# A fused RWKV attention and feed-forward block: the first tile's products with the state moved behind the second scores

## The chip, the cores and the metric

One core of a Trainium2 chip. The metric is device microseconds of one execution, median of three runs.

## The reference

Input x is 4 sequences of 2048 tokens with 512 channels. Two residual blocks follow each other, each on a layer norm of its input:

- Attention with a decaying state, 32 heads of 16 channels. r, k, v and a gate g are projections (512 x 512) of the normalized tokens mixed with the token before. A sequence is cut into chunks of 64 tokens. Per chunk and head: `att = (r k) * w_mat; y = att v + (r state) * wb; state = ws * state + (k * wk) v`. Then y is normalized per head, multiplied by silu(g) and projected by Wo.
- Feed-forward: `gelu(x W0' + b0) W1' + b1`, 512 to 2048 to 512, with half-precision roundings.

## The kernel before, in words

The 8192 tokens go through in 32 steps (n = 0 to 31) of 256 tokens, a step being two tiles (t) of 128 tokens, or four chunks (c) of 64. Three more steps drain the pipeline. Step n does the attention of block n, the tail (gate, Wo) of block n-1 and the feed-forward of block n-2; the down projection of block n-3 ends in it as well. Float32 operands are split into two halves of 16 bits (hi and lo), and a product is three matmuls (`PASSES`).

Each engine has one instruction stream, written out by hand, and works it off in order; semaphores order the engines among each other (`eng.wait_ge(s, count)`). From step 3 on the streams of VectorE and ScalarE are `dve_steady` (L1447) and `act_steady` (L1788); steps 0 to 2 use `dve_step` (L1534) and `act_step` (L1849). TensorE's is `pe_step` (L1174) for all of them. In steps 0 and 1 TensorE also prepares the feed-forward weights in 16 pieces (`pe_prepare`, L830).

What the change and the prediction speak of:

- The feed-forward pieces: `pe_up` (L1061), 16 matmuls each, counted 0 to 7 in the code ("up 4" to "up 7" here; the sixth piece is up 5). Pieces alternate between two banks of `F`, and from up 2 on each waits for the gelu of the piece two before it: `eng.wait_ge(s_h, NH * f + 2 * (j - 2) + 2)` (L1072). The gelus are ScalarE's `act_gelu` (L1773, L1785).
- The scores of a chunk: `pe_scores` (L940, L954), 32 small matmuls into `sc`; "second scores" are those of chunk 1. VectorE weighs them (`dve_weigh`, L1345, L1350), ScalarE makes the high half (`act_weights_hi`, L1736), VectorE the low half (`dve_weights_lo`, L1356), and TensorE multiplies weights with values (`pe_att_v`, L960, L976 and L979) per tile.
- The state: `pe_kv` (L1005) makes both chunks' products k v of a tile. VectorE masks each (`dve_state`, L1359, L1367) into `kv` and adds it to the faded state S (L1382). ScalarE makes the high half of S (`act_state_hi`, L1738), GpSimd the low half (`pool_state_lo`, L1985, L1988; semaphore `s_Sl`).
- "Products with the state": `pe_from_state` (L984, L995), 48 small matmuls per tile into `FROM_STATE`, the columns 0 to 255 and 768 to 1023 of the three banks of `YT`. `dve_take_y` (L1393) adds them to what `pe_att_v` left in `FROM_CHUNK`, the other columns. Before the change chunk 1's product k v lies in columns 768 to 1023 (`kv_place`, L1001).
- The gate's projection, in two halves: `pe_G` (L1031). The tail of block n-1: VectorE multiplies with the gate (`dve_gated`, L1311), ScalarE makes the high halves (`act_gated_hi`, L1724, "gated high halves"), GpSimd the low ones (`pool_gated_lo`, L1979), TensorE projects (`pe_Wo`, L1041).
- The next block's mixes: `dve_mix` (L272) and their high halves, `act_mix_hi` (L329, L335).

Of the kernel before, what the change touches and what calls it, by code (L numbers as in the profile page):

```python
# [8 lines left out]
ALU = mybir.AluOpType  # L9
# [4 lines left out]
C = 512  # L14
H, N = 32, 16
G = C // P
HID = 2048
Q = 64
BT, NT = 256, 2
NCH = BT // Q  # L20
# [16 lines left out]
def due(count):  # L37

    return not isinstance(count, int) or count > 0
# [55 lines left out]
def program(nc, ctx, a, consts, x, out, wd, nb):  # L95
# [67 lines left out]
    Y = YT[:, 0:2, :]  # L163
    T32 = YT[:, 2, :]
# [566 lines left out]
    kv = sb("kv", [P, C // 2])  # L731
    S = sb("S", [P, C // 2])
    Shl = sb("Shl", [P, 2, 2, C // 2], F16)
    yi = sb("yi", [P, C])
# [249 lines left out]
    def pe_from_state(eng, n, t):  # L984

        if n == 0 and t == 0:
            eng.wait_ge(s_zero, 2)
        if due(NCH * n + 2 * t + 1):
            eng.wait_ge(s_Sl, NCH * n + 2 * t + 1)
        for g in range(G):  # L990
            for i, (a, b) in enumerate(PASSES):
                for p in range(2):
                    for cc in range(2):
                        at = P * t + Q * cc
                        mm = eng.matmul(FROM_STATE[Q * cc:Q * cc + Q, rows_of(g, p).start // Q, Q * g:Q * g + Q],  # L995
                                        rT[rows_of(g, p), a, g, at:at + Q], Shl[rows_of(g, p), cc, b, Q * g:Q * g + Q],
                                        start=(i == 0), stop=(i == 2))
                        if g == G - 1 and i == 2 and p == 1:
                            mm.then_inc(s_in, 1)

    def kv_place(c):  # L1001

        return Y[:, 1, C // 2:C] if c % 2 else T32[:, 0:C // 2]

    def pe_kv(eng, n, t, ahead):  # L1005

# [24 lines left out]
    def pe_G(eng, n, half, ahead):  # L1031
        if half == 0:
            pe_mixed(eng, n, 3)
            eng.wait_ge(s_rl, 2 * n + 1)
            if ahead:
                eng.wait_ge(s_xT, NT * (n + 1) + 1)
        else:
            eng.wait_ge(s_gT, 2 * n + 1)
        pe_project_T(eng, B, G_, n, 3, half).then_inc(s_pG, 1)
# [134 lines left out]
    def pe_step(eng, n):  # L1174
        att_n, tail, ff, ahead, late = in_step(n)
        if n == nb:
            pe_after_attention(eng, n)
            return
        if n == nb + 2:
            pe_last_down(eng)  # L1180
            return
        if att_n and n != 1:
            pe_mixed(eng, n, 0)
            pe_K(eng, n, 0)
        if late:
            pe_down(eng, n - 3, 4)
        if att_n:
            pe_K(eng, n, 1)
        if late:
            pe_down(eng, n - 3, 5)  # L1190
        if att_n:
            pe_mixed(eng, n, 1)
            pe_R(eng, n, 0)
        if late:
            pe_down(eng, n - 3, 6)
        if att_n:
            pe_R(eng, n, 1)
            if n == 0:
                pe_piece_mean(eng, 0)
        if late:  # L1200
            pe_down(eng, n - 3, 7)
        if att_n:
            pe_mixed(eng, n, 2)
            pe_V(eng, n, 0)
            if n == 2:
                pe_V(eng, n, 1)
                pe_yT(eng, n)
            if n < STEADY:
                pe_next_X(eng, n)
            if n == 1:  # L1210
                pe_piece_mean(eng, 1)
            pe_prepare(eng, n, "X")
        if ff:
            pe_up(eng, n, 0)
        if att_n and n != 2:
            pe_V(eng, n, 1)
        if n == 1:
            pe_yT(eng, n)
        if att_n:
            pe_prepare(eng, n, "V1")  # L1220
        if ff:
            pe_up(eng, n, 1)
        if n > 2 and tail and not y_by_dma(n - 1):
            pe_yT(eng, n)
        if ff:
            pe_up(eng, n, 2)
        if ff:
            pe_up(eng, n, 3)
        if att_n:
            pe_scores(eng, n, 0)  # L1230
            pe_prepare(eng, n, "sc0")
            pe_kv(eng, n, 0, n < STEADY)
            pe_G(eng, n, 0, n < STEADY)
            pe_prepare(eng, n, "G0")
        if ff:
            pe_up(eng, n, 4)
        if att_n:
            pe_scores(eng, n, 1)
            pe_prepare(eng, n, "sc1")
        if ff:  # L1240
            pe_up(eng, n, 5)
        if att_n:
            pe_G(eng, n, 1, n < STEADY)
            pe_prepare(eng, n, "G1")
        if ff:
            pe_up(eng, n, 6)
        if att_n:
            pe_att_v(eng, n, 0)
        if ff:
            pe_up(eng, n, 7)  # L1250
        if att_n:
            pe_from_state(eng, n, 0)
            pe_scores(eng, n, 2)
            pe_prepare(eng, n, "sc2")
        if tail:
            pe_Wo(eng, n, 0)
            pe_prepare(eng, n, "Wo0")
        if ff:
            pe_down(eng, n - 2, 0)
        if att_n:  # L1260
            pe_kv(eng, n, 1, n < STEADY)
            pe_scores(eng, n, 3)
            pe_prepare(eng, n, "sc3")
        if n == 0:
            pe_mixed(eng, 1, 0)
            pe_K(eng, 1, 0)
        if ff:
            pe_down(eng, n - 2, 1)
        if tail:
            pe_Wo(eng, n, 1)  # L1270
        if ff:
            pe_down(eng, n - 2, 2)
        if att_n:
            pe_att_v(eng, n, 1)
            pe_from_state(eng, n, 1)
        if ff:
            pe_down(eng, n - 2, 3)
# [75 lines left out]
    def dve_weights_lo(eng, n, c):  # L1353
        for x in range(2):
            eng.wait_ge(s_ah, 8 * n + 2 * c + x + 1)
            eng.tensor_tensor(att[:, c % 2, 1, C * x:C * x + C], att32[:, x, :], att[:, c % 2, 0, C * x:C * x + C],  # L1356
                              ALU.subtract).then_inc(s_al, 1)

    def dve_state(eng, n, c):  # L1359
        eng.wait_ge(s_kv, NCH * n + c + 1)  # L1360
        if due(NCH * n + c):
            eng.wait_ge(s_S, NCH * n + c)
        dst = kv[:, :].rearrange("p (g c) -> p g c", g=G)
        src = kv_place(c).rearrange("p (g c) -> p g c", g=G)
        mask = headmask[:, :].unsqueeze(1).to_broadcast([P, G, 4 * N])
        if c < NCH - 1:
            eng.tensor_tensor(dst, src, mask, ALU.mult).then_inc(s_km, 1)  # L1367
        else:
            eng.scalar_tensor_tensor(out=dst, in0=src, scalar=flag[:, n + 1:n + 2], in1=mask,
                                     op0=ALU.mult, op1=ALU.mult).then_inc(s_km, 1)  # L1370
        eng.wait_ge(s_km, NCH * n + c + 1)
        fading = ws
        if c == NCH - 1:
            eng.wait_ge(s_wsf, n + 1)
            fading = wsf
        if due(NCH * n + c):
            eng.wait_ge(s_Sl, NCH * n + c)
        else:
            eng.wait_ge(s_zero, 1)
        for g in range(G):  # L1380
            at = slice(Q * g, Q * g + Q)
            last = eng.scalar_tensor_tensor(out=S[:, at], in0=S[:, at], scalar=fading[:, g:g + 1],  # L1382
                                            in1=kv[:, at], op0=ALU.mult, op1=ALU.add)
        last.then_inc(s_S, 1)

    def dve_gate(eng, n, half):
# [6 lines left out]
    def dve_take_y(eng, n, t):  # L1393
        eng.wait_ge(s_in, NCH * n + 2 * t + 2)
        eng.wait_ge(s_av, NCH * n + 2 * t + 2)
        if due(NT * n + t):
            eng.wait_ge(s_gs, NT * n + t)
        for x in range(2):
            at = slice(C // 2 * x, C // 2 * x + C // 2)
            last = eng.tensor_tensor(yi[:, at].rearrange("p (k a d) -> p a k d", a=2, d=N),  # L1400
                                     FROM_STATE[:, :, P * x:P * x + P].rearrange("p a (k d) -> p a k d", d=N)[:, ::1 - 2 * x],
                                     wb[:, H // 2 * x:H // 2 * x + H // 2].rearrange("p (k a) -> p a k", a=2).unsqueeze(3).to_broadcast(
                                         [P, 2, H // 4, N]), ALU.mult)
        last.then_inc(s_yi, 1)
        eng.wait_ge(s_yi, NT * n + t + 1)
        if due(NT * n):
            eng.wait_ge(s_yT, NT * n)
        halves = FROM_CHUNK.rearrange("p k (q b d) -> p k q b d", q=8, b=2)
        dst = y[:, t, :].rearrange("p (k q d) -> p k q d", k=2, q=8)
        sums = yi[:, :].rearrange("p (k q d) -> p k q d", k=2, q=8)  # L1410
        eng.tensor_tensor(sums, halves[:, :, :, 1, :], sums, ALU.add).then_inc(s_ylo, 1)
        eng.wait_ge(s_ylo, NT * n + t + 1)
        eng.tensor_tensor(dst, halves[:, :, :, 0, :], sums, ALU.add).then_inc(s_y, 1)
# [374 lines left out]
    def act_steady(eng, n, ahead):  # L1788
# [24 lines left out]
        act_gate(eng, n, 0)  # L1813
        act_state_hi(eng, n, 0)
        act_gated(eng, n - 1)
        act_weights_hi(eng, n, 1)
        act_gelu(eng, n, 4)
        act_gated_hi(eng, n - 1)
        if ahead:
            act_mix_hi(eng, n + 1, 0)  # L1820
# [436 lines left out]
```

## Time and profile before

| | |
|---|---|
| median of 3 runs | 2046.94 us (2045.29 to 2048.67) |
| profiled execution, its own time | 2050.78 us |
| profiled execution, span | 2049.0 us, granted clock 0.993 |
| TensorE busy | 1999.8 us (98%), 27206 matmuls |
| TensorE weight loads busy | 1424.3 us (70%) |
| VectorE busy | 1738.7 us (85%) |
| ScalarE busy | 1293.0 us (63%) |
| GpSimd busy | 317.5 us (15%) |
| chain that ended last | TensorE 81%, SyncE's queue 4%, VectorE 4%, ScalarE 4%, DMA 3%, issue 2% |
| granted TensorE clock over 40 slices | 0.8 in the first, 0.9 or more in all others |

Busy time is the union of an engine's instructions. The chain is followed back from the last instruction, at each step to what released it. A matmul's end is modelled, so TensorE is timed here by the starts of its instructions.

### The profile page before, as it was taken

The page shows a single profiled execution, that of the slowest core. Times are in us where ns is not written, and L with a number is a line of the kernel's source. Part 1 is how long each engine was busy: PE and PEld are TensorE (multiplying, and loading weights), DVE is VectorE, ACT ScalarE, POOL GpSimd, SP SyncE. Part 2 cuts the span into 40 slices and gives each one's busy share as a digit, 9 for nine tenths or more (in the row PEclk, how much of TensorE's full clock was granted, in tenths as well). Part 3 has the DMA queues.
Part 4 walks back from the last instruction along what each step waited for, and adds up shares of the span by engine and source line. Part 5 has one row for each costly group of instructions (what it writes and reads, how often), then busy time and mean ns, then how long its engine had stood idle before and what let it go on. Part 6 is the DMA issues. An engine that isn't in the chain of part 4 may idle for free.

```text
span 2049.0 us, 64453 instructions
## 1 busy us (share of the span) xinstructions
PE 1999.8 (98%) x27206; PEld 1424.3 (70%) x27206; DVE 1738.7 (85%) x3687; ACT 1293.0 (63%) x2081; POOL 317.5 (15%) x329
## 2 busy tenths in 40 slices
PE   5889999999999999999999999999999999999999
PEld 4767667777666777766777766667776677777676
DVE  7778889888888888888988888888888898888771
ACT  7775566676555677656667656667765666766452
POOL 1011111111111111111111111111111111111110
PEclk8999999999999999999999999999999999999999
DMA  6776666777666677766667766667777666776656
GB/s 217 161 193 194 177 178 182 199 197 196 177 194 171 189 198 195 185 190 189 173 194 202 199 174 186 181 181 202 192 195 184 191 180 185 199 202 177 181 175 191
DMA packets 403216, 385.42 MB, mean 188 GB/s; under 512 B 256880, under 2 KB 304112, under 8 KB 402928
## 3 DMA queue, kind: packets, MB, share of 16 engines
q1 hardware_dynamic: 401296, 381.12, 68.1%
q8 instruction: 215, 3.52, 0.7%
q14 instruction: 73, 0.60, 0.1%
q10 hardware_dynamic: 1632, 0.18, 0.1%
HBM read 232.32 MB, written 22.54 MB: 124 GB/s over the span
## 4 chain that ended last, share of the span: by engine, by line
PE 81%; SPq 4%; DVE 4%; ACT 4%; DMA 3%; issue 2%; POOL 0%; ACTq 0%; DVEq 0%
PE F L1149 19%; PE F L1086 16%; PE B L892 9%; PE B L1053 8%; PE sc L892 7%; PE YT L924 6%; PE YT L892 3%; DMA y<-ygT 3%; PE YT L976 3%; SPq L2044 2%; PE sc L954 2%; PE YT L995 2%; PE YT L1086 1%; PE F L847 1%; PE YT L1025 1%
## 5 line engine op out<-in xcount | busy, mean ns | idle before, releaser
L1149 PE MATMUL F<-ring,hT 128*128 128x512 f16 x1984 | 467.7, 379 | 0.5 <-issue 0.5
L1149 PEld LDWEIGHTS F<-ring,hT 128*128 128x128 f16 x1984 | 189.1, 98 | 198.4 <-issue 0.8
L1086 PE MATMUL F<-xT,kept 128*128 128x256 f16 x2400 | 276.8, 273 | 2.0 <-issue 1.2
L892 PE MATMUL B<-mix,WT 128*128 128x256 f16 x2304 | 267.5, 273 | 0.0
L1785 ACT ACTIVATE hT<-F,b,f_rho 128x256 f16<-128x256 f32 x480 | 243.4, 560 | 37.8 <-PE F L1086 37.7
L1086 PEld LDWEIGHTS F<-xT,kept 128*128 128x128 f16 x2400 | 234.6, 98 | 42.1 <-issue 2.6
L892 PEld LDWEIGHTS B<-mix,WT 128*128 128x128 f16 x2304 | 222.7, 98 | 33.3 <-DVE gT L1389 0.3
L279 DVE SCALAR_TENSOR_TENSOR mixf<-dx,maa,xnT 128x256 f32<-128x256 f32 x512 | 238.7, 527 | 0.1
L1742 ACT ACTIVATE Shl<-S 128x256 f16<-128x256 f32 x128 | 53.1, 415 | 236.2 <-PE YT L995 125.8
L1988 POOL TENSOR_TENSOR Shl<-S,Shl 128x256 f16<-128x256 f32 x128 | 89.2, 697 | 708.5 <-ACT Shl L1742 702.1
L1736 ACT ACTIVATE att<-att 128x512 f16<-128x512 f32 x256 | 147.5, 624 | 67.7 <-DVE att L1350 67.7
L339 DVE TENSOR_TENSOR mix<-mixf,mix 128x1024 f16<-128x1024 f32 x128 | 184.1, 1438 | 3.2 <-ACT mix L335 2.2
L892 PE MATMUL sc<-mix,WT 128*128 128x256 f16 x1536 | 180.4, 275 | 3.0 <-PEq L577 3.0
L1356 DVE TENSOR_TENSOR att<-att 128x512 f16<-128x512 f32 x256 | 166.8, 693 | 17.2 <-ACT att L1736 17.0
L924 PE MATMUL YT<-WT,mix 128*128 128x512 f16 x768 | 178.6, 383 | 1.3 <-DVE mix L339 0.9
L1086 PE MATMUL F<-xT,ring 128*128 128x256 f16 x1440 | 172.5, 273 | 4.1 <-ACT hT L1785 4.1
L1053 PE MATMUL B<-WT,yg 128*128 128x512 f16 x768 | 176.5, 379 | 0.0
L1350 DVE TENSOR_TENSOR att<-sc,wmask 128x512 f32<-128x512 f32 x256 | 164.3, 684 | 13.3 <-PE sc L954 13.1
L892 PEld LDWEIGHTS sc<-mix,WT 128*128 128x128 f16 x1536 | 151.0, 99 | 34.6 <-issue 3.6
L1993 POOL TENSOR_TENSOR x<-e,x 128x512 f32<-128x512 f16 x62 | 70.7, 1161 | 578.0 <-DVE e L1429 578.0
L1086 PEld LDWEIGHTS F<-xT,ring 128*128 128x128 f16 x1440 | 135.3, 98 | 23.3 <-issue 6.4
L335 ACT ACTIVATE mix<-mixf 128x1024 f16<-128x1024 f32 x128 | 134.6, 1051 | 5.1 <-DVE mixf L279 4.2
(208 smaller groups left out, 3108.6 us busy)
## 6 DMA issues: line engine op xcount, KB each, us to landing
ring<-w_dram SPq DMA_DIRECT2D x352, 512.0 KB, 3.7
kx<-kT SPq DMA_DIRECT2D x96, 256.0 KB, 3.8
rx<-rT SPq DMA_DIRECT2D x96, 256.0 KB, 4.5
xa<-in_L_attn_x SPq DMA_DIRECT2D x32, 512.0 KB, 5.0
vbd<-vN SPq DMA_DIRECT2D x256, 64.0 KB, 2.1
x<-in_L_attn_x SPq DMA_DIRECT2D x32, 512.0 KB, 5.0
out<-x SPq DMA_DIRECT2D x31, 512.0 KB, 3.5
kept<-in_L_ffn_W SPq DMA_DIRECT2D x5, 512.0 KB, 12.0
```

What stands on the lines that cost most here:

```text
L279: last = eng.scalar_tensor_tensor(out=mixf[:, m % 2, g, :], in0=dx[:, g, :], scalar=maa[:, m, g:g + 1], in1=xnT[:, g, 1:BT + 1], op0=ALU.m ...
L335: eng.activation(mix[:, m % 2, 0, :, :], mixf[:, m % 2, :, :], ACT.Copy).then_inc(s_mh, 1)
L339: eng.tensor_tensor(mix[:, m % 2, 1, :, :], mixf[:, m % 2, :, :], mix[:, m % 2, 0, :, :], ALU.subtract).then_inc(s_ml, 1)
L892: mm = eng.matmul(out[:, gg * BT:(gg + 1) * BT], WT[:, w, a, kk, rows(g)], mix[:, m % 2, b, kk, :], start=(i == 0 and kk == 0), stop=(i == ...
L924: mm = eng.matmul(Y[:, t, :], mix[:, 0, a, kk, rows(t)], WT[:, V_, b, kk, :], start=(i == 0 and kk == 0), stop=(i == 2 and kk == G - 1))
L1053: mm = eng.matmul(B[:, :], yg[:, a, kk, rows(t)], WT[:, O_, b, kk, :], start=(i == 0 and kk == 0), stop=(i == 2 and kk == G - 1))
L1086: mm = eng.matmul(up_place(f, j)[:, i * BT:(i + 1) * BT], w, xT[:, :, kk, :], start=(kk == 0 and a == 0), stop=(kk == G - 1 and a == 1))
L1149: mm = eng.matmul(F[:, t, :], hT[:, k, rows(t)], ring[:, use % RING, i, a * C:(a + 1) * C], start=(k == 0 and a == 0), stop=(k == NH - 1 a ...
L1350: eng.tensor_tensor(att32[:, x, :], sc[:, x, :], wmask[:, 8 * x:8 * x + 8, :].rearrange("p q i -> p (q i)"), ALU.mult).then_inc(s_am, 1)
L1356: eng.tensor_tensor(att[:, c % 2, 1, C * x:C * x + C], att32[:, x, :], att[:, c % 2, 0, C * x:C * x + C], ALU.subtract).then_inc(s_al, 1)
L1736: eng.activation(att[:, c % 2, 0, C * x:C * x + C], att32[:, x, :], ACT.Copy).then_inc(s_ah, 1)
L1785: eng.activation(hT[:, k, :], up_place(f, j)[:, i * BT:(i + 1) * BT], ACT.Gelu, bias=b0[:, k:k + 1], scale=f_rho[:, j:j + 1]).then_inc(s_h, 1)
```

## The change

- `pe_step`: the second scores go from behind up 4 to behind up 5, and the first tile's products with the state from behind up 7 to right behind the second scores. Up 6 and up 7 follow each other, and weights times values of the first tile comes behind up 7.
- `kv_place`: chunk 1's product k v goes to columns 256 to 511, out of `FROM_STATE`.
- `dve_state`: chunk 1's product is masked right behind chunk 0's fade, into the first half of `yi`; its fade stays where it was (`dve_fade`). `dve_take_y` of the first tile waits for that fade.
- `pe_from_state`: the first tile's also waits for chunk 1's mask.
- `act_steady`: gelu 4 goes ahead of the second scores' weights.

```diff
 def pe_from_state(eng, n, t):
-        if due(NCH * n + 2 * t + 1):
-            eng.wait_ge(s_Sl, NCH * n + 2 * t + 1)
+        if t == 0:
+            eng.wait_ge(s_km, NCH * n + 2)
+        eng.wait_ge(s_Sl, NCH * n + 2 * t + 1)
 def kv_place(c):
-        return Y[:, 1, C // 2:C] if c % 2 else T32[:, 0:C // 2]
+        return Y[:, 0, C // 2:C] if c % 2 else T32[:, 0:C // 2]
 def pe_step(eng, n):
             pe_up(eng, n, 4)
-        if att_n:
-            pe_scores(eng, n, 1)
-            pe_prepare(eng, n, "sc1")
         if ff:
             pe_up(eng, n, 5)
         if att_n:
+            pe_scores(eng, n, 1)
+            pe_from_state(eng, n, 0)
+            pe_prepare(eng, n, "sc1")
             pe_G(eng, n, 1, n < STEADY)
             pe_prepare(eng, n, "G1")
         if ff:
             pe_up(eng, n, 6)
+            pe_up(eng, n, 7)
         if att_n:
             pe_att_v(eng, n, 0)
-        if ff:
-            pe_up(eng, n, 7)
-        if att_n:
-            pe_from_state(eng, n, 0)
             pe_scores(eng, n, 2)
+    def masked(c):
+        return yi[:, 0:C // 2] if c == 1 else kv[:, :]
 def dve_state(eng, n, c):
+        if c == 1:
+            dve_fade(eng, n, c)
+            return
...
+        dve_fade(eng, n, c)
+        if c == 0:
+            eng.wait_ge(s_kv, NCH * n + 2)
+            if due(n):
+                eng.wait_ge(s_gs, NT * n)
+            eng.tensor_tensor(masked(1).rearrange("p (g c) -> p g c", g=G),
+                              kv_place(1).rearrange("p (g c) -> p g c", g=G), mask, ALU.mult).then_inc(s_km, 1)
+    def dve_fade(eng, n, c):
...
-                                            in1=kv[:, at], op0=ALU.mult, op1=ALU.add)
+                                            in1=masked(c)[:, at], op0=ALU.mult, op1=ALU.add)
 def dve_take_y(eng, n, t):
+        if t == 0:
+            eng.wait_ge(s_S, NCH * n + 2)
 def act_steady(eng, n, ahead):
         act_gated(eng, n - 1)
+        act_gelu(eng, n, 4)
         act_weights_hi(eng, n, 1)
-        act_gelu(eng, n, 4)
         act_gated_hi(eng, n - 1)
```

## Rows read from the trace of the kernel before

**Rows 1.** Waits of TensorE, 255 to 1960 us: total, times, longest.
```profile
PE F L1086 <- ACT hT L1785: 4.1, 8, 0.7
```
**Rows 2.** Timeline of TensorE, step 22: start, length, engine, line, form, count.
```profile
1403.96 0.45 PE L954 MATMUL sc<-rx,kx 64*64 64x64 f16 x32
...
1409.26 0.45 PE L954 MATMUL sc<-rx,kx 64*64 64x64 f16 x32
1409.64 1.92 PE L1086 MATMUL F<-xT,ring 128*128 128x256 f16 x16
1411.40 2.78 PE L892 MATMUL B<-mix,WT 128*128 128x256 f16 x24
1414.02 1.91 PE L1086 MATMUL F<-xT,ring 128*128 128x256 f16 x16
1415.86 0.22 PE L976 MATMUL YT<-vbd,att 128*64 128x64 f16 x2
...
1416.98 1.92 PE L1086 MATMUL F<-xT,ring 128*128 128x256 f16 x16
1418.83 0.58 PE L995 MATMUL YT<-Shl,rT 64*64 64x64 f16 x48
1419.23 0.46 PE L954 MATMUL sc<-rx,kx 64*64 64x64 f16 x32
1419.63 2.76 PE L1053 MATMUL B<-WT,yg 128*128 128x512 f16 x12
...
1464.01 0.45 PE L954 MATMUL sc<-rx,kx 64*64 64x64 f16 x32
```
**Rows 3.** Timeline of ScalarE, step 22, from the gated high halves to gelu 5.
```profile
1413.19 1.16 ACT L1729 ACTIVATE yg<-ygT 128x512 f16<-128x512 f32 x2
1414.23 1.06 ACT L335 ACTIVATE mix<-mixf 128x1024 f16<-128x1024 f32 x1
1415.18 1.02 ACT L1785 ACTIVATE hT<-F,b,f_rho 128x256 f16<-128x256 f32 x2
```
**Rows 4.** Timeline of VectorE, step 22.
```profile
1404.46 1.29 DVE L1350 TENSOR_TENSOR att<-sc,wmask 128x512 f32<-128x512 f32 x2 [0.28 <-PE sc L954]
...
1410.29 1.28 DVE L1350 TENSOR_TENSOR att<-sc,wmask 128x512 f32<-128x512 f32 x2
1411.49 1.29 DVE L1315 TENSOR_TENSOR ygT<-ygT,gT 128x512 f32<-128x512 f32 x2
```
**Rows 5.** Timeline of GpSimd, step 22.
```profile
1409.48 0.83 POOL L1988 TENSOR_TENSOR Shl<-S,Shl 128x256 f16<-128x256 f32 x1 [5.99 <-ACT Shl L1742]
```
**Rows 6.** Timeline of ScalarE, step 26: its gelu 5.
```profile
1656.79 1.00 ACT L1785 ACTIVATE hT<-F,b,f_rho 128x256 f16<-128x256 f32 x2
```
**Rows 7.** Timeline of TensorE, step 26: second scores and up 7.
```profile
1649.53 0.44 PE L954 MATMUL sc<-rx,kx 64*64 64x64 f16 x32
...
1658.00 1.92 PE L1086 MATMUL F<-xT,ring 128*128 128x256 f16 x16
```
**Rows 8.** Timeline of GpSimd, steps 0, 1 and 2: low half of the state.
```profile
84.90 0.67 POOL L1988 TENSOR_TENSOR Shl<-S,Shl 128x256 f16<-128x256 f32 x1 [14.30 <-ACT Shl L1742]
...
147.00 1.12 POOL L1988 TENSOR_TENSOR Shl<-S,Shl 128x256 f16<-128x256 f32 x1
...
204.64 1.12 POOL L1988 TENSOR_TENSOR Shl<-S,Shl 128x256 f16<-128x256 f32 x1
```
**Rows 9.** Timeline of TensorE, steps 0, 1 and 2.
```profile
72.42 2.04 PE L847 MATMUL F<-xT,kept 128*128 128x128 f32 x8 [2.27 <-ACT vw L828]
...
83.34 1.13 PE L847 MATMUL F<-xT,kept 128*128 128x128 f32 x8 [0.83 <-ACT kept L862]
...
142.53 1.13 PE L847 MATMUL F<-xT,ring 128*128 128x128 f32 x8 [0.83 <-ACT ring L862]
...
202.85 2.78 PE L892 MATMUL B<-mix,WT 128*128 128x256 f16 x24
```
**Rows 10.** Busy times in a window: length, engines with counts, PEclk, DMA share, GB/s.
```profile
72.40:75.80 3.40, 3.38 (x17) 3.34 (x18) 3.40 (x9) 1.29 (x3) 0.00 (x0) 0.50 0.98 108
```

More of the change, by code:

```diff
@@ L1362, in dve_state @@
             eng.wait_ge(s_S, NCH * n + c)
-        dst = kv[:, :].rearrange("p (g c) -> p g c", g=G)
+        if c == 1:
+            dve_fade(eng, n, c)
+            return
+        dst = masked(c).rearrange("p (g c) -> p g c", g=G)
         src = kv_place(c).rearrange("p (g c) -> p g c", g=G)
```

## The prediction

> **What bounds the kernel now.** I read the page's engine shares and its chain that ended last first: TensorE is busy 98% of the span and holds 81% of the chain, so the kernel is its in-order queue, and any wait put into that queue is added to the time. Next the waits of TensorE over the 28 steps n = 3 to 30, which are alike: 8 waits, 4.1 us in all, each of a feed-forward piece for a gelu that must empty the PSUM bank it will overwrite [rows 1]. So there is almost nothing to win by removing waits, and the change must be read as a new order in a full queue. For that I took one undisturbed step, n = 22, engine by engine: the reader is to see TensorE without a gap [rows 2], and beside it VectorE and ScalarE, whose order is fixed too and runs only a little ahead of it [rows 3, 4]. The step lasts 60.05 us (1403.96 to 1464.01).
>
> **The change part by part, in step 22.** Times count from the start of the second scores before the change (1409.26).
>
> *TensorE's order.* Before: second scores, up 5, gate half, up 6, weights times values, up 7, products with the state, third scores, Wo. After: up 5, second scores, products with the state, gate half, up 6, up 7, weights times values, third scores, Wo. No matmul is added or taken away. Up 5 takes 1.76 (1409.64 to 1411.40), the gate half 2.62, an up piece ahead of a large group 1.75 (its 1.76, rounded down), one ahead of a small group 1.85 (1416.98 to 1418.83), weights times values 1.12, the group of products and scores 0.40 + 0.40 [rows 2]. If nothing waits, the new order has the second scores at 1.76, the gate half at 2.56, up 6 at 5.18, up 7 at 6.93, weights times values at 8.78, third scores at 9.90 and Wo at 10.30. Before, Wo began at 10.37. So the regrouping alone gives 0.07 us a step: one group of small matmuls less has to be entered and left.
>
> The row for that: an up piece that is followed by a small group takes 0.09 longer than one that isn't [rows 2]. The Trainium skill, TensorEngine Tiling (Array Packing), section Key Properties, says that changing the tiling mode drains the engine. By that rule fewer changes of mode mean less time, and the change would be a gain; the trace agrees in sign.
>
> *The moved VectorE work.* The mask of chunk 1's product (0.42 us, same size) moves ahead of the mixes; it has its own destination, so nothing is computed twice. It makes VectorE reach the gate half 0.42 later, but it then still waits for the second scores: it would be ready at 1410.29 + 0.42, 1.45 after the mark, and the scores let it start at 2.26 (below). Cover 0.8 us, cost nothing.
>
> *The new waits of the products.* They need the low half of the state from GpSimd: ready at 1409.48 + 0.83, so at 1.05 after the mark, wanted at 2.16 [rows 5, 2]. Cost nothing in such a step; the mask they also wait for is earlier still.
>
> *What the second scores now hold up.* This is where it goes wrong. Up 7 writes the bank of up 5, so it waits for gelu 5. By `act_steady` after the change ScalarE runs gelu 4, the weights of the second scores, the gated high halves, the next block's mix, gelu 5 (the last three in [rows 3]); the edit swaps only the first two. The gated high halves wait for VectorE's gating, which stands in VectorE's queue behind the weighing of the second scores [rows 4]. So gelu 5 hangs on the second scores, which are now 1.76 later, though nothing in it needs them. Step by step: the weighing starts 0.50 after its scores start (1404.46 against 1403.96) [rows 2, 4], at 2.26. Gating starts 1.20 later (1410.29 to 1411.49), at 3.46, and takes 1.29, to 4.75. Take 0.05 for the signal, between no time and 0.1: high halves at 4.80. From there the spacings of the rows: 1.04 to the mix, 0.95 to gelu 5, 1.02 for gelu 5 itself, so it ends at 7.81, and up 7 starts at 7.85. It could have started at 6.93: TensorE waits 0.92. Before, gelu 5 ended at 1416.20 and up 7 started at 1416.98, so there were 0.78 to spare; both sides of the slack move against it. From up 7 on: 1.85 + 1.12 + 0.40 to Wo, at 11.22 against 10.37, **+0.85 us a step**. Later in the step nothing pays it back: Wo and the down pieces have no waits to shorten [rows 1].
>
> *Steps in which ScalarE is late.* In 8 of the 28 [rows 1] ScalarE got to its gated work late and up 6 waited for gelu 4, which is why gelu 4 is put ahead of the weights: that wait goes, 4.1 us. But what is ahead of gelu 5 is the same work in another order. In step 26 it ends at 1656.79 + 1.00 as before [rows 6], so up 7 starts at about 1657.84 instead of 1658.00 [rows 7], and from there to Wo it is 3.37 now and was 2.65 (1416.98 to 1419.63): +0.56.
>
> Sum of the steady steps: 20 x 0.85 + 8 x 0.56 = **21.5 us**.
>
> *Steps 0, 1 and 2.* There the products' wait is not covered. The low half of the state is ready at 85.57, 148.12 and 205.76 (start and duration of GpSimd's row; in steps 1 and 2 it also stands behind the gated low halves) [rows 8]. What TensorE now does after the second scores began at 83.34, 142.53 and 202.85 [rows 9]; with the products between (0.5) it begins at 86.1, 148.7 and 206.3, so 2.8, 6.1 and 3.4 later. Off go the products at their old place, 0.5 each as an estimate (0.40 and 0.09 of [rows 2]). That is 2.3 + 5.6 + 2.9 = **10.8 us**. The chain of waits runs through TensorE, ScalarE and VectorE there with little idle, so I take all of it; bounds 0 (all absorbed) and 14 (nothing taken off).
>
> *The clock.* After an idle time of 2.27 TensorE started at 72.42, and the stretch 72.4 to 75.8 had a granted clock of 0.50 [rows 9, 10]: 1.2 instead of 2.4 GHz, so about 1.7 us of 3.4 are lost. The new idle times are about 3.1, 6.5 and 2.9 us long. Bounds 0 and 3 x 1.7; I take two of the three, **3.4 us**. The 0.9 us of the steady steps should do nothing: the waits before were up to 0.7 [rows 1] and the page has full clock throughout.
>
> Sum: 21.5 + 10.8 + 3.4 = 35.7. The profiled execution (2050.78 by its own time) would become 2086.5. It lies 3.8 above the median of the runs, 2046.94, to which the sum is added for the forecast: **2082.6 us**.
>
> **The rivals.**
> 1. *Only the steady wait shows.* The early steps' idle is taken back by waits behind it, where ScalarE, VectorE and GpSimd catch up. For: the chain there changes engine every few microseconds. Against: TensorE's share of it is large, and its next steps start late. 21.5 alone: 2068.
> 2. *The wait feeds on itself.* ScalarE gets to its work late in every step, as in step 26, because transfers shift with the longer step. There gelu 5 ended 8.26 after the start of the second scores (1649.53) [rows 6, 7]; with 0.05 for the signal up 7 then starts at 8.31, not 7.85. 20 x 0.46 = 9.2 more, with the whole sum 44.9: 2092. Against: the late steps come from a DMA ahead of the moved work, and a longer step gives it more time.
> 3. *Faster: only the regrouping counts.* Mechanism: fewer groups of small matmuls, at 0.07 a step, and up 6 no longer waits. 28 x 0.07 + 4.1 = 6: 2041. It holds from the point at which gelu 5 ends by 6.9 after the mark, 0.9 earlier than worked out, and the early steps cost nothing. For it speaks 0.09 in the rows; against it the fixed order of ScalarE. This is the case that the skill's rule on modes leads to.
> 4. *A wash*: the steady steps gain 6 as in the third and the early steps pay 10.8: 2052 at most, about no change.
>
> **How the numbers follow.** Forecast 0.60, rival 1 0.18, rival 2 0.12, rival 3 0.05, rival 4 0.05. The forecast's own range is 2074 to 2089: steady 18 to 23, early 8 to 14, clock 0 to 5. The range of 8 in 10 takes in rivals 1 and 2, less about 0.08 at their far ends: 2062 to 2093. About 0.2% (4.1 us) can be told from no change. Faster 0.04, same 0.05, slower 0.91.
>
> **What would show it.** In the waits of TensorE after: up pieces waiting for gelu some 28 times, 0.7 to 0.95 each, 20 to 30 us in all, where 8 waits had 4.1. In a step: the wait stands ahead of up 7, none ahead of the products, and gelu 5 ends 0.05 before up 7 starts. ScalarE idle ahead of the gated high halves, with VectorE's gating as releaser. In steps 0 to 2: the products wait for GpSimd's low half. The period of an undisturbed step: 60.9. I am wrong if up 7 follows up 6 without a gap (then gelu 5 doesn't hang on the second scores), or if the products wait for the state in steady steps.

## The result

The changed kernel takes 2083.0 us (median of 6 runs, 2082.48 to 2085.58), the kernel before 2048.03 us (6 runs): ratio 1.0174, 95% interval 1.0163 to 1.0185. It is 35 us slower; 35.7 us were forecast. The profiled execution took 2082.48 us by its own time (span 2080.7 us, before 2049.0).

The page of the changed kernel, its engine shares: about as much TensorE work as before (1999.8 us, 98%) in a longer span.

```profile
PE 2001.7 (96%) x27206; PEld 1428.6 (69%) x27206; DVE 1746.3 (84%) x3687; ACT 1296.4 (62%) x2081; POOL 331.3 (16%) x329
```

The waits of TensorE from 250 to 2000 us, the steady steps. L1087 is the feed-forward piece, L1801 the gelu, L996 the products with the state, L2004 GpSimd's low half of the state. [rows 1] had 4.1 us in 8 waits:

```profile
PE F L1087 <- ACT hT L1801: 24.6, 28, 1.1
PE YT L996 <- POOL Shl L2004: 0.2, 1, 0.2
```

And from 60 to 260 us, steps 0 to 2, the first row of the answer:

```profile
PE YT L996 <- POOL Shl L2004: 11.9, 3, 6.6
```

So both waits are where the prediction put them. Step 22 after the change, TensorE, to be held against [rows 2]:

```profile
1427.71 0.44 PE L954 MATMUL sc<-rx,kx 64*64 64x64 f16 x32
...
1433.00 1.91 PE L1087 MATMUL F<-xT,ring 128*128 128x256 f16 x16
1434.84 0.44 PE L954 MATMUL sc<-rx,kx 64*64 64x64 f16 x32
1435.11 0.62 PE L996 MATMUL YT<-Shl,rT 64*64 64x64 f16 x48
1435.67 2.79 PE L892 MATMUL B<-mix,WT 128*128 128x256 f16 x24
1438.30 1.91 PE L1087 MATMUL F<-xT,ring 128*128 128x256 f16 x16
1441.06 1.91 PE L1087 MATMUL F<-xT,ring 128*128 128x256 f16 x16 [0.86 <-ACT hT L1801]
...
1488.77 0.45 PE L954 MATMUL sc<-rx,kx 64*64 64x64 f16 x32
```

VectorE in the same step, against [rows 4]: the weighing waits for the second scores, the gating follows.

```profile
1435.33 1.29 DVE L1348 TENSOR_TENSOR att<-sc,wmask 128x512 f32<-128x512 f32 x2 [0.89 <-PE sc L954]
1436.54 1.28 DVE L1313 TENSOR_TENSOR ygT<-ygT,gT 128x512 f32<-128x512 f32 x2
```

ScalarE, against [rows 3]: idle ahead of the gated high halves until VectorE's gating, then the mix and gelu 5.

```profile
1437.91 1.15 ACT L1745 ACTIVATE yg<-ygT 128x512 f16<-128x512 f32 x2 [0.63 <-DVE ygT L1313]
1438.97 1.04 ACT L335 ACTIVATE mix<-mixf 128x1024 f16<-128x1024 f32 x1
1439.92 1.00 ACT L1801 ACTIVATE hT<-F,b,f_rho 128x256 f16<-128x256 f32 x2
```

The reader is to see one chain: scores 1434.84, weighing 1435.33, gating 1436.54 to 1437.82, high halves 1437.91, mix, gelu 5 to 1440.92, up 7 at 1441.06. By the spacing of [rows 2] up 7 was wanted 1.75 after up 6, at 1440.05, so TensorE lost 1.01; the row's 0.86 counts from the modelled end of up 6.

Step 22 lasts 61.06 us here, 0.08 more than an undisturbed step of the changed kernel, and that 0.08 lies ahead of up 4 (which starts 3.54 after the first scores, 3.46 in step 22 before the change). Two first scores that are 60.98 apart, of steps 24 and 25:

```profile
1549.85 0.45 PE L954 MATMUL sc<-rx,kx 64*64 64x64 f16 x32
...
1610.83 0.45 PE L954 MATMUL sc<-rx,kx 64*64 64x64 f16 x32
```

Steps 0 to 2, TensorE, the products with the state:

```profile
83.38 0.57 PE L996 MATMUL YT<-Shl,rT 64*64 64x64 f16 x48 [3.21 <-POOL Shl L2004]
...
148.81 0.85 PE L996 MATMUL YT<-Shl,rT 64*64 64x64 f16 x48 [6.55 <-POOL Shl L2004]
...
213.61 0.57 PE L996 MATMUL YT<-Shl,rT 64*64 64x64 f16 x48 [2.11 <-POOL Shl L2004]
```

The granted clock behind these waits, by windows (length, then busy time of TensorE, its weight loads, VectorE, ScalarE and GpSimd, then PEclk):

```profile
84.90:88.30 3.40, 3.40 (x22) 3.15 (x20) 0.27 (x2) 0.49 (x1) 0.00 (x0) 0.50 0.09 27
146.30:153.20 6.90, 4.39 (x66) 4.29 (x67) 2.71 (x6) 0.06 (x1) 2.37 (x2) 0.51 0.02 6
214.60:218.00 3.40, 3.40 (x19) 2.42 (x17) 1.93 (x6) 0.76 (x2) 0.00 (x0) 0.50 0.02 5
```

The second of these stretches begins inside the wait, which ends at 148.81, so TensorE has only 4.39 us of work in it. The wait of 2.27 us in step 0, behind which the kernel before had half clock ([rows 9], [rows 10]), is there after the change too, but the clock behind it is 1.00 (71.7 to 76.0), and the same 8 matmuls take 1.13 us instead of 2.04:

```profile
71.72 1.13 PE L847 MATMUL F<-xT,kept 128*128 128x128 f32 x8 [2.27 <-ACT vw L828]
```

Counted by the starts of the first scores, steps 3 to 30 take 1709.2 us together, 1690.0 before: +19.2. Steps 0 to 2 take 61.83, 72.61 and 64.43, before 60.57, 65.02 and 60.41: +12.9. The start is 0.7 earlier and the end 0.3 longer: 31.7, the difference of the two spans. The medians differ by 3.3 more than these two executions. Step 0 of the kernel before can account for most of that: in the eight executions of this document that have TensorE's old order there, it takes 57.7 to 57.9 us in four, with full clock at 72 us, and 60.0 to 60.6 in four, with half clock there, and this execution is one of the latter.

### The profile page after: what moved, and what is told of

Read it like the earlier page. It is cut to its first block, busy times and chain, and to the rows that moved or that the text cites. A ratio compares the mean times of both kernels' runs of the same rounds, so it can differ in the third digit from the quotient of the medians.

```text
span 2080.7 us, 64546 instructions
## 1 busy us (share of the span) xinstructions
PE 2001.7 (96%) x27206; PEld 1428.6 (69%) x27206; DVE 1746.3 (84%) x3687; ACT 1296.4 (62%) x2081; POOL 331.3 (16%) x329
## 4 chain that ended last, share of the span: by engine, by line
PE 82%; DVE 5%; ACT 4%; issue 3%; DMA 1%; SPq 1%; POOL 0%; ACTq 0%; DVEq 0%
PE F L1150 20%; PE F L1087 17%; PE B L892 8%; PE B L1054 8%; PE sc L892 8%; PE YT L924 7%; PE YT L892 4%; PE YT L976 2%; PE sc L954 2%; DVE ygT L1313 1%; ACT mix L335 1%; PE F L847 1%; PE YT L1087 1%; PE YT L1026 1%; ACT hT L1801 1%
## 5 line engine op out<-in xcount | busy, mean ns | idle before, releaser
L1087 PE MATMUL F<-xT,kept 128*128 128x256 f16 x2400 | 276.8, 273 | 2.0 <-issue 1.2
L1801 ACT ACTIVATE hT<-F,b,f_rho 128x256 f16<-128x256 f32 x480 | 244.3, 563 | 38.1 <-PE F L1087 38.0
L1087 PEld LDWEIGHTS F<-xT,kept 128*128 128x128 f16 x2400 | 234.6, 98 | 42.1 <-issue 2.7
L2004 POOL TENSOR_TENSOR Shl<-S,Shl 128x256 f16<-128x256 f32 x128 | 96.0, 750 | 715.0 <-ACT Shl L1758 715.0
L1087 PE MATMUL F<-xT,ring 128*128 128x256 f16 x1440 | 171.6, 272 | 24.9 <-ACT hT L1801 24.9
L1054 PE MATMUL B<-WT,yg 128*128 128x512 f16 x768 | 176.5, 379 | 0.0
L1354 DVE TENSOR_TENSOR att<-att 128x512 f16<-128x512 f32 x256 | 166.4, 692 | 10.8 <-ACT att L1752 10.7
L1087 PEld LDWEIGHTS F<-xT,ring 128*128 128x128 f16 x1440 | 138.7, 98 | 48.1 <-issue 32.4
```

Source lines behind the costliest of these rows:

```text
L1054: mm = eng.matmul(B[:, :], yg[:, a, kk, rows(t)], WT[:, O_, b, kk, :], start=(i == 0 and kk == 0), stop=(i == 2 and kk == G - 1))
L1087: mm = eng.matmul(up_place(f, j)[:, i * BT:(i + 1) * BT], w, xT[:, :, kk, :], start=(kk == 0 and a == 0), stop=(kk == G - 1 and a == 1))
L1801: eng.activation(hT[:, k, :], up_place(f, j)[:, i * BT:(i + 1) * BT], ACT.Gelu, bias=b0[:, k:k + 1], scale=f_rho[:, j:j + 1]).then_inc(s_h, 1)
```

## The experiments

The theory: gelu 5 stands on ScalarE behind work that hangs on the second scores, and these now come one feed-forward piece later; in steps 0 to 2 the products with the state wait for GpSimd. The rivals: the new order costs something by itself (the products ahead of the gate half, or up 7 right behind up 6), or the idle time is there whatever the order. Line numbers shift by some lines with the edits; medians of the kernel before differ by up to 4.5 us between the groups of runs, so the ratios decide.

**Gelu 5 first.** The changed kernel with

```diff
         act_gelu(eng, n, 4)
+        act_gelu(eng, n, 5)
         act_weights_hi(eng, n, 1)
         act_gated_hi(eng, n - 1)
         if ahead:
             act_mix_hi(eng, n + 1, 0)
-        act_gelu(eng, n, 5)
```

> The changed kernel with one edit on ScalarE: gelu 5 directly behind gelu 4, ahead of the second scores' weights and the gated high halves. Theory (gelu 5 hangs on the second scores through the weighing, the gating and the gated high halves): TensorE's wait ahead of up 7 goes, an undisturbed step goes from 60.98 us to about 60.0, 28 steps give back 27 us, 2056 us; steps 0 to 2 stay as slow. Rival (the next wait stands right behind, since the gated high halves and the low halves for Wo now come after one gelu more): the wait moves ahead of Wo or of weights times values, over 2075 us.

2061.53 us, 1.0058 of before (1.0039 to 1.0078). Up 6 and up 7 now run as one piece of 32 matmuls. TensorE in a step of this run, 1425 to 1431 us:

```profile
1425.99 3.66 PE L1087 MATMUL F<-xT,ring 128*128 128x256 f16 x32
```

No up piece waits for a gelu any more; an undisturbed step takes 60.02. But the rival has a share. The waits of TensorE in the steady steps (L1054 is Wo, L1403 the gate half that VectorE reads out of the bank that Wo writes):

```profile
PE B L1054 <- DVE gT L1403: 6.8, 9, 0.8
PE YT L996 <- POOL Shl L2004: 1.4, 3, 0.5
```

The 9 steps are those in which ScalarE starts its gated work over 0.7 us late; their wait has moved on. The two rows come to 8.2 us, enough for the 5.5 us above the 2056 expected (4 by the ratio, since the kernel before was 1.5 slower in these runs).

**The old order in steps 0 to 2.** The changed kernel with the products and the second scores at their old places where `n < STEADY`:

```diff
+        old = n < STEADY
+        if att_n and old:
+            pe_scores(eng, n, 1)
+            pe_prepare(eng, n, "sc1")
         if ff:
             pe_up(eng, n, 5)
-        if att_n:
+        if att_n and not old:
             pe_scores(eng, n, 1)
             pe_from_state(eng, n, 0)
-            pe_prepare(eng, n, "sc1")
...
+            if old:
+                pe_from_state(eng, n, 0)
             pe_scores(eng, n, 2)
```

> The changed kernel with TensorE's old order in steps 0 to 2 alone (second scores behind up 4, products with the state behind up 7). Theory: the products no longer wait for GpSimd's low half of the state there; the three steps took 12.9 us longer in the trace, so 2070 us, and the steady steps stay at 60.98. Rival (that idle time is mostly taken back or is the clock's and comes anyway): 2078 us or more.

2070.22 us, 1.0096 (1.0080 to 1.0112), with 28 waits of 24.6 us in the steady steps as before the edit. The early cost is as large as the trace showed: 12.8 us by the medians, 16 by the ratios. Step 0 itself differs between executions (57.9 here, 60.6 in the kernel before), so a single pair of traces gives the cost to about 3 us: steps 0 to 2 of the changed kernel are 15.3 longer than here, 12.9 longer than before the change.

**Both edits.**

> Both edits together: gelu 5 behind gelu 4, and the old order in steps 0 to 2. Theory: the two costs are all that the change costs and they add; what is left is the regrouping, 0.07 us a step, and the wait of up 6 for gelu 4 that goes (4.1 us): 2042 us, 0.997 of before. Rival (the new order costs something of its own, in the matmuls or in the queue): 2050 us or more.

2047.49 us, 0.9989 (0.9979 to 0.9999), 5 us above the expectation and short of the rival. The two costs add within the intervals (by the ratios the edits give back 1.16% and 0.78% one by one and 1.85% together), and what is left of the change is a gain at the edge of what can be told. An undisturbed step takes 60.01 to 60.02 where it took 60.05: the regrouping is worth 0.04 us, not 0.07. The first scores of steps 23 and 24, 60.02 apart:

```profile
1460.57 0.44 PE L954 MATMUL sc<-rx,kx 64*64 64x64 f16 x32
...
1520.59 0.45 PE L954 MATMUL sc<-rx,kx 64*64 64x64 f16 x32
```

The 4.1 us of up 6 are not won, for the late steps wait elsewhere:

```profile
PE B L1054 <- DVE gT L1413: 5.0, 8, 0.8
```

**Gelu 4 back.**

```diff
-        act_gelu(eng, n, 4)
         act_weights_hi(eng, n, 1)
+        act_gelu(eng, n, 4)
         act_gated_hi(eng, n - 1)
```

> The changed kernel with gelu 4 back behind the second scores' weights on ScalarE. Theory: the weights now wait for the later scores, gelu 4 ends about 10.4 us after the first scores, the gated high halves start at 10.35 instead of 10.12, and up 7 waits 0.23 longer in each of 28 steps: 2089 us; up 6 about as before. Rival (ScalarE's order of these two makes no difference, as the gating sets the high halves): 2083 us.

2093.25 us, 1.0201 (1.0180 to 1.0221). TensorE's waits in the steady steps are 28 as in the changed kernel, 0.11 longer each on average:

```profile
PE F L1087 <- ACT hT L1801: 27.7, 28, 1.1
```

An undisturbed step takes 61.15 instead of 60.98, so the swap that came with the change saves 0.17 of the 0.23 expected, 4.8 us in 28 steps; by the ratios it is 5.5. The medians are 10 us apart; 3.8 of that lie in steps 0 to 2 of this execution, where nothing was edited.

**Which of the two moves?** First the second scores back behind up 4, the products alone moved, behind up 5 (steps 0 to 2 in the old order, ScalarE as changed):

```diff
             pe_up(eng, n, 4)
+        if att_n:
+            pe_scores(eng, n, 1)
         if ff:
             pe_up(eng, n, 5)
         if att_n:
-            pe_scores(eng, n, 1)
             pe_from_state(eng, n, 0)
```

> Steady steps: the second scores stay behind up 4 as before the change, only the products with the state move, behind up 5; up 6 and up 7 adjacent; steps 0 to 2 in the old order; ScalarE as in the changed kernel. Theory (it is the scores' later place that holds up gelu 5, not the products): gelu 5 ends 12.3 us after the first scores, up 7 is wanted at 12.4 and waits 0.1 at most, so 2046 to 2049 us. Rival (the products ahead of the gate half, or up 7 right behind up 6, cost it): 2065 us or more.

2052.66 us, 1.0020 (1.0009 to 1.0031), 4 us above the expectation but far from the rival. An undisturbed step takes 60.13, 0.08 more than before the change, without a wait ahead of up 7: the products stand alone between two large groups here, and the next group starts 0.51 us behind them, where it was 0.40 with the third scores behind them [rows 2]. The late steps show again:

```profile
PE F L1087 <- ACT hT L1810: 6.8, 9, 1.0
```

So the products ahead of the gate half and up 7 behind up 6 cost 0.08 us a step together, not 0.9: it is the place of the second scores that holds TensorE up. Then the products right behind the scores at up 4:

```diff
             pe_scores(eng, n, 1)
+            pe_from_state(eng, n, 0)
         if ff:
             pe_up(eng, n, 5)
-        if att_n:
-            pe_from_state(eng, n, 0)
```

> Steady steps: second scores behind up 4 and the products with the state right behind them there, then up 5, gate half, up 6, up 7; steps 0 to 2 in the old order; ScalarE as in the changed kernel. Theory (the low half of the state comes 6.3 to 6.7 us after the first scores, TensorE wants it at 5.7): TensorE waits 0.7 to 1.0 us for GpSimd in each of 28 steps, and no longer for gelu 5: 2068 to 2075 us. Rival (the state is there in time, as in the changed kernel): 2047 us.

2075.67 us, 1.0139 (1.0124 to 1.0155), just above the expected range. All steady waits are for GpSimd's low half, and they are a little longer than expected, 1.2 us on average:

```profile
PE YT L996 <- POOL Shl L2013: 34.2, 29, 2.0
```

The pair of scores and products is thus caught between two chains: at up 4 it is too early for the state, behind up 5 it is too late for gelu 5 as ScalarE was ordered.

**GpSimd's order in steps 1 and 2.** The changed kernel with chunk 0's low half of the state ahead of the gated low halves:

```diff
-        if tail and not y_by_dma(n - 1):
+        if tail and not att_n:
             pool_gated_lo(eng, n - 1)
...
-                if c == 0 and tail and y_by_dma(n - 1):
+                if c == 0 and tail:
                     pool_gated_lo(eng, n - 1)
```

> The changed kernel with GpSimd's low half of chunk 0's state ahead of the gated low halves in steps 1 and 2, as it is in the steady steps. Theory (in these two steps the products wait for the state half that stands behind the gated low halves): it is ready some 3.7 us earlier in step 1 and 2.5 to 3 in step 2; 2077 us. Rival (the state itself is late there, through VectorE and ScalarE): 2083 us.

2075.45 us, 1.0133 (1.0119 to 1.0147). In step 1 the half stands ready 14.2 us after the first scores instead of 17.8, so 3.6 earlier, and over steps 0 to 2 the products wait 6.1 us instead of 11.9. What is left, 3.2 in step 0 and 2.9 in step 1, is the rival's share: there GpSimd itself waits for ScalarE's high half. GpSimd in step 1, in the changed kernel and here, and below it the wait of the products, 60 to 260 us:

```profile
144.88 2.71 POOL L1998 TENSOR_TENSOR yg<-ygT,yg 128x512 f16<-128x512 f32 x2 [14.78 <-ACT yg L1745]
147.55 1.11 POOL L2004 TENSOR_TENSOR Shl<-S,Shl 128x256 f16<-128x256 f32 x1
```

```profile
143.68 0.67 POOL L2004 TENSOR_TENSOR Shl<-S,Shl 128x256 f16<-128x256 f32 x1 [14.26 <-ACT Shl L1758]
144.31 2.72 POOL L1998 TENSOR_TENSOR yg<-ygT,yg 128x512 f16<-128x512 f32 x2
```

```profile
PE YT L996 <- POOL Shl L2004: 6.1, 2, 3.2
```

**Can the late steps be had as well?** Three orders of the steady steps, each on top of both edits. First the second gate half earlier on both engines:

```diff
         act_weights_hi(eng, n, 1)
+        act_gate(eng, n, 1)
         act_gated_hi(eng, n - 1)
...
-        act_gate(eng, n, 1)
...
         dve_weights_lo(eng, n, 1)
+        dve_gate(eng, n, 1)
         dve_state(eng, n, 1)
         if ahead:
             mix_lo(eng, n + 1, 0)
-        dve_gate(eng, n, 1)
```

> The kernel with both edits (gelu 5 behind gelu 4, old order in steps 0 to 2), and the second gate half ahead of the gated high halves on ScalarE and ahead of chunk 1's fade on VectorE. Theory (in steps in which ScalarE is late, Wo now waits for the gate half that VectorE reads out of the bank last, 5.0 us in 8 steps): those waits go, 2042.5 us, 0.997 of before. Rival (the late steps only move their wait on, to the gated low halves): 2047 us as without this edit.

2049.67 us, 1.0007 (0.9998 to 1.0016): the theory fell. The waits for the gate half are gone, yet an undisturbed step is 60.27. VectorE now waits for ScalarE's tanh ahead of chunk 1's fade and is 0.3 later from there on; the second Wo, which needs VectorE's first residual, starts 22.84 after the first scores instead of 22.59. The row of TensorE's waits shows only the longest of these delays:

```profile
PE B L1054 <- DVE x L1328: 2.2, 4, 0.6
```

Then the low halves of the next block's mixes one place later each:

```diff
         dve_state(eng, n, 1)
-        if ahead:
-            mix_lo(eng, n + 1, 0)
         dve_gate(eng, n, 1)
         dve_take_y(eng, n, 0)
         dve_weigh(eng, n, 2)
         if ahead:
-            mix_lo(eng, n + 1, 1)
+            mix_lo(eng, n + 1, 0)
         dve_weights_lo(eng, n, 2)
         dve_variance(eng, n, 0)
         dve_residual(eng, n - 1, 0)
+        if ahead:
+            mix_lo(eng, n + 1, 1)
```

> The kernel with both edits (gelu 5 behind gelu 4, old order in steps 0 to 2), and on VectorE in steady steps the two low halves of the next block's mixes one place later each: the first behind the weighing of the third scores, the second behind the first residual. ScalarE as with both edits. Theory (in late steps VectorE is behind by the work that stands ahead of the gate half and of the first tile's y; nobody needs the low halves for another 15 us): the waits of Wo for the gate half, 5.0 us in 8 steps, go and no new one comes, 2042 to 2044 us, 0.997 to 0.998 of before. Rival (VectorE has no room in these steps whatever the order, as when the gate half was put ahead: the wait moves to the first residual or to the weights of the fourth scores): 2047 us or more.

2067.02 us, 1.0084 (1.0070 to 1.0098): the theory fell. Ahead of chunk 2's state VectorE has no room; weights times values of the second tile waits for the mask of chunk 3 in every step:

```profile
PE YT L976 <- DVE kv L1384: 24.9, 28, 0.9
```

The place with room is behind chunk 3's fade, where VectorE waited 1.1 us anyway:

```diff
         dve_residual(eng, n - 1, 0)
-        if ahead:
-            mix_lo(eng, n + 1, 1)
         dve_state(eng, n, 2)
         dve_weigh(eng, n, 3)
         dve_weights_lo(eng, n, 3)
         dve_state(eng, n, 3)
         if ahead:
+            mix_lo(eng, n + 1, 1)
             dve_take_y(eng, n, 1)
```

> As the run before, but the second low half of the next block's mixes stands behind chunk 3's fade on VectorE, where VectorE is idle for 1.1 us ahead of the second tile's y. Theory (the wait of 0.9 us for chunk 3's mask was these 1.2 us of low half standing ahead of it): that wait goes, and with it the late steps' wait for the gate half; undisturbed steps 60.0 us, 2042 to 2045 us, 0.997 to 0.9985 of before. Rival (VectorE's y of the second tile comes too late then, and the next step's start with it): 2050 us or more.

2039.54 us, 0.9943 (0.9926 to 0.9960): better than forecast, and the one version that clearly beats both kernels. In the steady steps next to nothing is left to wait for, and an undisturbed step takes 59.96:

```profile
PE YT L996 <- POOL Shl L2013: 0.6, 3, 0.2
PE YT L1087 <- DMA xT<-xh: 0.5, 1, 0.5
```

How much of this the kernel before would have gained from VectorE's new order alone was not tried.

## Why the prediction was right

- *The chain to gelu 5* is right step by step: moving gelu 5 out of it removes the wait, and so does moving the second scores back. Its size was a little low: an undisturbed step went from 60.05 to 60.98, +0.93 for 0.85 forecast; 0.92 of wait were forecast and 1.01 came. The steps taken from rows fit (weighing 0.49 after its scores, gating 1.21 later, 1.06 to the mix, 0.95 to gelu 5); the guessed 0.05 for a signal was short, 0.09 from VectorE to ScalarE (1437.82 to 1437.91) and 0.14 from ScalarE to TensorE (1440.92 to 1441.06).
- *The sum of the steady steps* is 19.2 for 21.5. Here two errors met. 28 x 0.93 would be 26.0; but the kernel before had 8.6 us of its own above 28 x 60.05 (late steps and single stops), and the changed one only 1.8 above 28 x 60.98. Late steps all but vanished, where 8 were assumed at 0.56 each. ScalarE still starts its gated work late in nine steps, but in an undisturbed step it now idles 0.63 us ahead of the gated high halves, and a late start comes out of that idle time. In step 26 it starts 0.45 late, and the step lasts 60.98. ScalarE there, waiting for a transfer, and the idle time that is left:

```profile
1673.29 2.56 ACT L1738 ACTIVATE ygT<-y 128x1024 uint16<-128x1024 uint16 x2 [0.34 <-DMA y<-ygT]
...
1681.94 1.15 ACT L1745 ACTIVATE yg<-ygT 128x512 f16<-128x512 f32 x2 [0.30 <-DVE ygT L1313]
```

  The rival in which the wait feeds on itself is refuted by this: it goes the other way.
- *Regrouping*: 0.04 us a step, shown with both costs away, for 0.07. The rival that went by the fewer groups alone (6 us) had the sign right; with both costs away 0.1% is left (0.01 to 0.21), about 2 us, since its 4.1 us of up 6 were not to be had without more work on VectorE.
- *Steps 0 to 2*: 12.9 us in the trace and 13 to 16 in the run that undoes them, for 10.8 and 3.4 of the clock. The waits are 3.21, 6.55 and 2.11 us long, for 3.1, 6.5 and 2.9 forecast. The rival that they are absorbed is refuted. The clock term was sized too small: half clock came behind all three waits and not two, and in the second for longer. TensorE is busy 3.40, 4.39 and 3.40 us in these stretches, so by an estimate (half the work of full clock) 5.6 us are lost, not 3.4. The trace hides a part of it, because the kernel before had half clock at 72 and 120 us for 3.4 us longer each, and there the executions with the old order differ among themselves too. The row that the term was read from doesn't carry it alone: the same wait of 2.27 us has full clock behind it after the change. That GpSimd's order is part of it is shown by the 7.6 us that its swap gives back (8.4 by the ratios), of which 5.8 are the wait.
- *VectorE's moved mask and the products' wait for the state in steady steps* cost nothing, as said: VectorE is idle 0.89 ahead of the weighing, and one wait of 0.2 is all that the products have.
- *The total* lies within 1 us of the forecast, and that is in part luck. By the ratios the steady steps cost 20 us and the early ones 16, for 21.5 and 14.2: one error of about 2 us too much and one of about 2 us too little.

## What to carry to other kernels

In a full in-order queue a step that is moved later takes with it all that other engines have queued behind its consumers; follow their written order to the next thing that the full engine needs, and move that thing ahead in the same edit. Count the first iterations apart: their order on the helping engines can differ, and here 3 of 32 steps made over a third of the loss. The place for displaced work is where an engine waits anyway, not the next gap in the code.

## What the runs showed of the hardware

VectorE's four fades of chunk 1's state take 0.86 to 0.87 us in steps 0 to 2 of the kernel with both edits, where GpSimd is idle meanwhile, and 2.69 in step 26, while GpSimd's gated low halves run (1653.18, 2.34 long). VectorE in step 2, the four fades as one row:

```profile
205.67 0.86 DVE L1406 SCALAR_TENSOR_TENSOR S<-S,ws,yi 128x64 f32<-128x64 f32 x4
```

VectorE in step 26, the four fades one by one, and GpSimd's two instructions:

```profile
1653.30 1.18 DVE L1406 SCALAR_TENSOR_TENSOR S<-S,ws,yi 128x64 f32<-128x64 f32 x1
1654.41 1.19 DVE L1406 SCALAR_TENSOR_TENSOR S<-S,ws,yi 128x64 f32<-128x64 f32 x1
1655.53 0.27 DVE L1406 SCALAR_TENSOR_TENSOR S<-S,ws,yi 128x64 f32<-128x64 f32 x1
1655.72 0.27 DVE L1406 SCALAR_TENSOR_TENSOR S<-S,ws,yi 128x64 f32<-128x64 f32 x1
```

```profile
1653.18 1.22 POOL L2008 TENSOR_TENSOR yg<-ygT,yg 128x512 f16<-128x512 f32 x1 [4.66 <-ACT yg L1755]
1654.37 1.16 POOL L2008 TENSOR_TENSOR yg<-ygT,yg 128x512 f16<-128x512 f32 x1
```

The Trainium skill, SBUF — State Buffer, section "SBUF: two separate sides", says that a VectorE operation with two SBUF inputs and a GpSimd operation that reads SBUF exclude each other on a shared pair of ports: the one that starts first holds it to its end, and the other waits. The trace agrees: the first two fades, 1.18 and 1.19 us long, each end 0.08 behind one of GpSimd's two instructions (1654.48 and 1654.40, 1655.60 and 1655.52), and the other two, behind both, take 0.27 each. It is part of why VectorE has so little room there.

A stop of 0.9 us in every step left the granted clock at 1.00 from 218 us to the last step, while a stretch at 0.50 goes with each of the three stops of 2.1 to 6.6 us. The length of one stop alone doesn't tell, though: 2.27 us ahead of the same matmuls had 0.50 behind it in the kernel before and 1.00 in the changed one.
